# Six transposes of the identity ahead of each of TensorE's last thirteen pieces, in a gated cross-attention layer on one core

## The reference

```python
x = x + tanh(g_xattn[0]) * xattn(layernorm(x), ctx_512, Wq, w_kc_q, w_kc_kv, W_qr, W_kr, Wo)
x = x + tanh(g_ffn[0]) * ffn(layernorm(x), router_weight, router_bias, expert_bias)

# ffn, per token
logits = flat @ router_weight.T + router_bias      # 64 experts
scores = softmax(logits)
topk_w, topk_idx = top_k(scores, 8)
out = flat * sum(topk_w) + einsum('tk,tkh->th', topk_w, expert_bias[topk_idx])
```

## Time and profile before

| what | us |
|---|---|
| median of 3 runs | 306.44 |
| lowest and highest | 304.74, 307.68 |
| span of the profiled execution | 306.0 |
| TensorE busy | 286.0 (93%) |
| VectorE busy | 195.0 (64%) |
| ScalarE busy | 150.6 (49%) |
| GpSimd busy | 135.4 (44%) |

### The profile page before, as it was taken

How to read it: one execution, slowest core, us unless ns; L and a number is a source line. 1 busy time by engine, 2 the same in 40 slices (tenths; PEclk the granted TensorE clock), 3 DMA queues, 4 the chain that set the end, 5 groups by cost and what they waited for, 6 DMA issues and landing times.

```text
span 306.0 us, 5002 instructions
## 1 busy us (share of the span) xinstructions
PE 286.0 (93%) x1672; PEld 207.7 (68%) x1672; DVE 195.0 (64%) x454; ACT 150.6 (49%) x451; POOL 135.4 (44%) x210
## 2 busy tenths in 40 slices
PE   7899799999998999999998999999989997899786
PEld 7883587487746786678657784778467844768463
DVE  3686896377726765567547862777368735677664
ACT  1402655475238363664456363852473627656332
POOL 2856068325732555037613743257416742333103
PEclk9999999999999999999999999999999997999975
DMA  8972030035000000450000000000000000001012
GB/s 227 384 205 77 1 87 2 1 126 159 2 0 0 2 2 0 122 163 2 0 0 2 1 0 2 0 0 3 0 2 2 0 2 0 0 2 34 2 36 69
DMA packets 13787, 13.17 MB, mean 43 GB/s; under 512 B 4226, under 2 KB 13122, under 8 KB 13634
## 3 DMA queue, kind: packets, MB, share of 16 engines
q1 hardware_dynamic: 13234, 12.46, 13.3%
q10 hardware_dynamic: 528, 0.39, 0.4%
HBM read 11.80 MB, written 1.05 MB: 42 GB/s over the span
## 4 chain that ended last, share of the span: by engine, by line
PE 75%; DVE 13%; issue 4%; ACT 3%; POOL 3%; DMA 1%; ACTq 0%; DVEq 0%; POOLq 0%
PE ring L884 21%; PE context L1005 9%; PE ring L894 8%; PE probs_t L993 7%; PE scores L982 6%; DVE q_stack L651 6%; PE ring L922 6%; PE ring L905 5%; PE scores L983 4%; PE ring L959 2%; PE ring L854 2%; ACT q_stack L572 2%; PE ring L945 1%; PE ring L862 1%; DMA x_sb<-in_x 1%
## 5 line engine op out<-in xcount | busy, mean ns | idle before, releaser
L481 POOL TENSOR_SCALAR probs<-probs,inv_sum 128x256 f32<-128x256 f32 x128 | 59.9, 483 | 108.5 <-DVE inv_sum L800 108.5
L447 POOL TENSOR_TENSOR roped<-roped,cross 128x512 f32<-128x512 f32 x48 | 60.7, 1286 | 29.6 <-DVE cross L665 29.5
L581 ACT ACTIVATE probs<-scores,neg_max 128x256 f32<-128x256 f32 x128 | 60.0, 479 | 12.2 <-DVE neg_max L794 11.9
L591 ACT COPY probs_t_sb<-probs_t 128x512 f32<-128x512 f32 x64 | 37.8, 591 | 52.6 <-PE probs_t L993 52.5
L794 DVE TENSOR_REDUCE neg_max<-scores 128x2 f32<-128x512 f32 x64 | 43.4, 679 | 7.0 <-PE scores L983 7.0
L982 PE MATMUL scores<-keys_hi,q_stack 128*128 128x256 f32 x128 | 40.1, 335 | 7.4 <-DVE q_stack L651 4.9
L651 DVE TENSOR_TENSOR q_stack<-ring,q_stack 64x512 fp32r<-64x512 f32 x32 | 22.0, 688 | 30.8 <-ACT q_stack L572 30.3
L664 DVE TENSOR_TENSOR roped<-ring,rope_q_sb 128x512 f32<-128x512 f32 x48 | 33.0, 688 | 11.9 <-PE ring L884 11.0
L982 PEld LDWEIGHTS scores<-keys_hi,q_stack 128*128 128x128 f32 x128 | 24.3, 190 | 23.5 <-issue 14.2
L884 PE MATMUL ring<-xn_hi,a_hi 128*128 128x512 f32 x96 | 39.1, 407 | 0.9 <-DVE a_lo L651 0.6
L993 PE MATMUL probs_t<-ident,probs 128*128 128x128 f32 x256 | 39.0, 275 | 0.8 <-POOL probs L481 0.5
(11 more groups left out here) (90 smaller groups left out, 447.0 us busy)
## 6 DMA issues: line engine op xcount, KB each, us to landing
wq_sb<-in_wq SPq DMA_DIRECT2D x4, 512.0 KB, 4.7
wo_t_sb<-in_wo_t SPq DMA_DIRECT2D x4, 512.0 KB, 4.9
w_qr_sb<-in_w_qr SPq DMA_DIRECT2D x4, 384.0 KB, 3.3
rope_q_sb<-in_rope_q SPq DMA_DIRECT2D x1, 1536.0 KB, 8.8
w_kc_q_sb<-in_w_kc_q SPq DMA_DIRECT2D x3, 384.0 KB, 4.6
x_sb<-in_x SPq DMA_DIRECT2D x4, 256.0 KB, 6.8
w_kr_sb<-in_w_kr SPq DMA_DIRECT2D x4, 192.0 KB, 3.7
out<-x_sb SPq DMA_DIRECT2D x3, 256.0 KB, 2.2
```

What stands on the lines that cost most here:

```text
L447: last = nc.gpsimd.tensor_tensor(roped[:, j, k, :], roped[:, j, k, :], cross[:, done % 2, j, :], ALU.add)
L481: last = nc.gpsimd.tensor_scalar(e, e, inv_sum[:, i % 4, half:half + 1], 1.0, ALU.mult, ALU.mult)
L581: last = nc.scalar.activation(probs[:, i % E_BUFS, half, :], scores[:, i % 2, half, :], ACT.Exp, bias=neg_max[:, i % 4, half:half + 1], ac ...
L591: nc.scalar.copy(probs_t_sb[:, i % T_BUFS], probs_t[:]).then_inc(probs_t_ready, 1)
```

## The change

Each bank-taking piece of `pieces_after` behind the first four entries (`out`, `out`, `turn` 4, `part` 2) gets six transposes of the identity ahead of its waits. They write the first 128 columns of the scores bank, which nothing reads any more, and they wait for nothing and signal nothing. There are 13 such pieces, so 78 transposes. No other engine's program changes.

```diff
 WARM_UP = 40
 LEAD = 2
+KEEP_WARM = 6
...
+            def keep_warm():
+
+                for _ in range(KEEP_WARM):
+                    nc.tensor.transpose(scores[:, 0, 0, 0:P], ident[:], ident[:])
+
-            def pieces(slot):
+            def pieces(slot, warm=False):
                 for u, piece in slot:
                     if piece[0] in NO_BANK:
                         continue
+                    if warm:
+                        keep_warm()
                     free(u)
...
-            pieces(after)
+            pieces(after[:4])
+            pieces(after[4:], warm=True)
```

## The result

| | before | changed |
|---|---|---|
| median of 4 runs | 307.06 us | 310.95 us |
| lowest and highest | 304.74, 307.94 | 309.72, 311.32 |
| ratio | | 1.0145, 95% interval 1.0092 to 1.0199 |
| profiled execution, span | 306.0 | 309.1 |
| mean granted clock | 0.975 | 0.994 |

The account below looks back on a forecast made before the run. TensorE was taken to bound the tail: 8.22 us work, 8.50 transposes and 0.90 changes of kind sum to 17.62, ending 3.70 later. Span 306.0 + 3.7 = 309.7, plus 0.44 to the median: 310.1 us, range 307.9 to 312.4.

Parts of the forecast that it names:

- TensorE sets the end, and each transpose is paid in full: In the tail, 78 transposes at 0.109 us each cost 8.50 us; TensorE ends 3.70 us later.
- The sum of the tail: TensorE from 289.43 us: real work 8.22, new transposes 8.50, changes of kind 0.90, together 17.62 us.
- the change of kind: Extra 0.15 us when transposes follow `logit` 4, `mix` 2, `logit` 6, `logit` 7, `mix` 4 or `mix` 6: 0.90 us.
- The clock holds: TensorE's granted clock stays at 2.4 GHz from 260 us to the end, thought likely but not sure.
- the stretch near 256 us: TensorE at 1.2 GHz from 256.55 to 259.96 us, ahead of the tail; being spared it was worth 1.6 us.
- No waits of TensorE left: In the new tail TensorE waits for nobody; before, it had three waits, 1.6 us in all.
- What is bought and what is paid: In the tail, at most 5.7 us won back from lower clock and waits, against 9.4 us put in.
- From the span to the time: Span 309.7 us; the profiled execution was taken as 0.44 us under the median, giving 310.1 us.
- the fourth rival: Execution shown may not stand for the median; tail or 256.55 us stretch differs: 308.5 us, at most 1% slower, chance 0.15.
- One stretch at half clock: First rival: clock falls once around `logit` 4 to `mix` 2 or `logit` 6 and 7, costing 1.6: 311.7 us, chance 0.20.
- The clock falls and stays: Clock falls at 294.1 us as before and stays at half to the end: 321.8 us, chance 0.03.
- The waits hide the transposes: At the end, transposes run free in TensorE's waits while VectorE's chain sets the end: 304.0 us, chance 0.06.

Follow-up runs that it names:

- three filled waits: Changed kernel with transposes only ahead of `logit` 4 (five), `logit` 6 (three) and `pick` 6 (six): 0.9897 of the kernel before, 0.9969 on another chip.
- the 16 transposes: 16 transposes in TensorE's wait ahead of the last step's first scores; with none in the tail, 306.20 us, ratio 0.9973 to the kernel before.
- the last three kernels: Against the kernel before: five transposes ahead of `logit` 4 only, 0.9991; three filled waits plus the 16 transposes, 0.9913 and 0.9922; the 16 transposes alone, 0.9973.
- four filled waits: The three filled waits plus the 16 transposes: 304.08 us, ratio 0.9913 to the kernel before; on another chip 304.20 us, 0.9922.

## Why the prediction was right, point by point

**That TensorE sets the end, and each transpose is paid in full: right.** Doubling them made the tail 8.51 us longer, and the sum had 8.50 for 78. The pitch of 0.109 us from the start of the kernel holds in the tail.

**The sum of the tail: 17.62 us, measured 17.26.** The term that was mis-sized is the change of kind. The sum had 0.15 us behind `logit` 4, 6 and 7 as well; the chain shows six transposes with 0.66 or 0.67 behind logits and 0.80 or 0.81 behind `mix` only. Three times 0.15 is 0.45 too much. `mix` 6 and 7 took 0.63 and 0.64 instead of 0.6 each. 17.62 − 0.45 + 0.07 = 17.24.

**The clock holds: right** in the profiled execution, and by their mean clocks in all four (0.994 three times and 0.997; the stretch near 256 us alone makes 0.994), and in the profiles with three and with twelve transposes too. The rule of the Trainium skill that transposes do not engage the full clock ("TensorE: Matmul & The Clock Gate", Part 4) isn't borne out: by the prediction's layout it would have made the tail 24.6 us long instead of 12.95 from 294.1 on, and 0.50 was granted nowhere in it. But real products ran between the transposes.

**No waits of TensorE left: right**, 17.24 of 17.26 us busy. GpSimd's three additions took from 301.68 to 304.33, 0.6 earlier than laid out (the whole tail began 0.27 earlier), and released nothing late.

**What is bought and what is paid.** The prediction had 5.7 us to win (3.4 for the clock, 2.3 for waits) and 9.4 to pay. With the mis-sized term mended, 9.0 are paid, and the tail grew by 17.26 − 13.92 = 3.34, so some 5.6 were won. The profile of the kernel with three filled waits shows what is left when the work is put where TensorE waits: its last addition starts 2.57 us earlier than that of before, and there the other engines, not TensorE, are the limit. In some of its runs the clock fell all the same.

**From the span to the time: the step that was off.** The prediction put the profiled execution of before 0.44 us under the median. The runs of the experiments show spans 1.8 us under the time of their own run (306.51 with 304.7, 307.88 with 306.1), and the four of the changed kernel 1.8 to 2.4. So that execution, at a span of 306.0 and a clock of 0.975, would by my estimate be one of about 307.8 us, above the median and not near 306.44. Adding 3.7 to that gives 311.5; the changed kernel's profiled execution took 311.32. The forecast of 310.1 leant on a median of three runs out of a spread of 3 us, and the new median of before is 307.06; the forecast's difference of 3.7 us stands against 3.9 measured.

That the two differences agree so well is in part luck. Between the two profiled executions the spans grew by 3.1 us: 3.34 in the tail, less the 0.27 by which the changed one reached its tail earlier. The 3.9 is a difference of two medians of four runs, of which those of before lie 3.2 us apart.

**The range.** Its ends were said to be the fourth rival and the first with half a microsecond each. That gives 308.0 to 312.2; the 307.9 to 312.4 on record are a little wider. 310.95 lies inside both.

**The rivals.** *One stretch at half clock* did not show in the tail of the changed kernel. *The clock falls and stays* did not either, but it is what one dense product in place of six transposes mostly did. *The waits hide the transposes* fell with the twelve: nothing was hidden. *The execution shown may not stand for the median* was in part true, in the other direction: by the estimate above it was slower than the median, not faster in its tail. One of the four runs, 309.72 us at 0.997, is 0.9 to 1.6 us under the others. The prediction gave 1.6 to the stretch near 256 us; the mean clock says that this run was spared it, though it was not profiled.

**What stays open:** what decides in which execution the clock falls. The traces hold a hint at the kernel's start, where the program is the same in all of them. The 40 transposes there take the less time the sooner the clock comes up. They took 6.94 to 7.40 us in the eight profiled executions that have the stretch near 256 us, and 6.09 to 6.86 in the five that don't. The kernel before and the one with the dense product, neither of which has anything new near 256 us:

```profile
1.68 7.34 PE L1014 MATMUL scores<-ident 128*128 128x128 f32 x40 [1.68 <-POOL ident L420]
1.68 6.29 PE L1022 MATMUL scores<-ident 128*128 128x128 f32 x40 [1.68 <-POOL ident L421]
```

So where the clock falls late in the kernel goes with when it came up at the start, and that differs between executions. This is a match over thirteen traces and not an experiment; three of the five also had the 16 transposes. No run brought the clock down in the tail and then added transposes, so whether they would bring it back there was not seen.

## What to carry to other kernels

Work that only keeps TensorE's clock up is paid in full on a chain that TensorE sets: put it in the waits of that engine, size it to the wait, and compare its own time with what the half clock costs. Here 78 transposes lost 1.45%, 39 won 0.4%, 14 in three waits won 1.0% once and 0.3% or nothing the second time, and 30 in four waits won 0.8 to 0.9% both times. Compare several executions by mean granted clock before believing one profile, since a kernel near the edge has runs 3 us apart, and cover all its thin places together: one alone changed little here.

## What was not expected of the hardware

- The clock of TensorE is a matter of the execution: of the 25 runs of the kernel before that stand beside the last three kernels, the times go from 304.42 us at a mean clock of 0.988 to 308.88 at 0.968, and nearly all in order of their clock. 0.020 of the mean over 305 us is 12.2 us more at half clock, for 4.46 us of time: 0.37 us lost for each microsecond at half clock.
- The spread of the runs itself nearly went when the waits were filled: 3.6 us in eighteen runs of the kernel before, 0.44 us in seven of the one with four filled waits. But of the eight runs on the other chip three lost some clock again, two a little (305.33 and 305.53 us) and one much (308.86), so the cover isn't complete.
- TensorE at 14.75 of 14.76 us busy stayed at 1.2 GHz (one dense product ahead of each piece), while it was granted 2.4 GHz at 17.24 of 17.26 with six transposes ahead of each.
